# A two-layer attention and expert kernel: the split of the row maxima moves from VectorE to GpSimd, and product slices change places

## What is computed

```python
x = x + layernorm(attn(layernorm(x)))      # 16 heads of 16, causal, window of 250 keys
x = x + layernorm(ffn(layernorm(x)))
# ffn(src): second attention (16 heads, no mask, k and v by way of 64 columns)
#   x  = rmsnorm(src + attention @ Wo) * norm1_w
#   shared = swiglu(x @ W_shared_in) @ W_shared_out
#   w  = weights of the two best of 4 experts in the chosen group of 2
#   h  = swiglu(x @ W1_shared);  routed = sum_e (h @ W2_experts[e]) * w[:, e]
#   out = rmsnorm(x + shared + routed) * norm2_w
```

## Time and profile before

| | us |
|---|---|
| runs of the kernel before | 1979.39, 1984.70, 1986.41 |
| median | 1984.70 |
| the profiled execution's own time | 1978.52 |
| its span | 1976.8 |

### The profile page before, as it was taken

The page is one execution under the profiler, slowest core; times in us unless marked ns, Lnnn a source line. Parts: engine busy times, 40 slices in busy tenths (PEclk is TensorE's granted clock), DMA queues, the critical chain, the costliest instruction groups (busy, mean ns, idle before and its releaser), DMA issues.

```text
span 1976.8 us, 27875 instructions
## 1 busy us (share of the span) xinstructions
PE 1833.7 (93%) x9216; PEld 1022.6 (52%) x9216; DVE 1345.6 (68%) x4116; ACT 807.6 (41%) x1730; POOL 382.1 (19%) x671
## 2 busy tenths in 40 slices
PE   7968899989999999999999999998999999999988
PEld 4343464636555364644637355463645537364466
DVE  6457474775768668685876857677586856868466
ACT  3433535245343634335353353425534363443510
POOL 2336024101231013200251011410123101320010
PEclk8585999999999999999999999899999999999999
DMA  3026002201031100401022010220103110040240
GB/s 110 2 84 236 23 22 87 86 2 54 23 139 44 44 22 13 163 20 48 29 97 87 2 54 23 97 85 2 54 23 139 44 44 23 26 157 1 97 170 11
DMA packets 31295, 123.04 MB, mean 62 GB/s; under 512 B 5424, under 2 KB 18352, under 8 KB 26544
## 3 DMA queue, kind: packets, MB, share of 16 engines
q1 hardware_dynamic: 28624, 105.54, 14.9%
q0 software_dynamic: 2528, 15.73, 2.1%
HBM read 101.33 MB, written 18.87 MB: 61 GB/s over the span
## 4 chain that ended last, share of the span: by engine, by line
PE 74%; DVE 17%; issue 5%; ACT 3%; DMA 1%; POOL 0%; SPq 0%; DVEq 0%; ACTq 0%; POOLq 0%
PE fb L852 12%; PE ot L791 10%; PE sm L750 8%; PE fb L830 6%; DVE negmax L1232 6%; PE st L777 5%; PE fb L826 4%; PE st L718 3%; PE dn L718 3%; PE fb L848 3%; PE st L734 3%; DVE sm L1229 2%; DVE acc L1430 2%; PE sm L777 2%; PE ot L718 2%
## 5 line engine op out<-in xcount | busy, mean ns | idle before, releaser
L630 ACT ACTIVATE probs<-st 128x512 f32<-128x512 f32 (+3 forms) x832 | 395.4, 507 | 388.1 <-PE st L777 384.4
L852 PE MATMUL fb<-w_r,h_r 128*128 128x512 f32 x1344 | 391.5, 418 | 0.0
L750 PE MATMUL sm<-k_t,q_t 48*128 48x512 f32 (+3 forms) x864 | 313.8, 447 | 63.8 <-DVE negmax L1229 31.1
L1232 DVE TENSOR_REDUCE negmax<-sm 128x1 f32<-128x512 f32 x416 | 268.8, 685 | 83.5 <-PE sm L750 83.4
L777 PE MATMUL st<-q_t,k_t 64*128 64x512 f32 (+3 forms) x832 | 298.7, 453 | 22.3 <-ACT probs L630 19.9
L750 PEld LDWEIGHTS sm<-k_t,q_t 48*128 48x128 f32 x864 | 144.5, 195 | 315.3 <-DVE negmax L1229 136.5
L852 PEld LDWEIGHTS fb<-w_r,h_r 128*128 128x128 f32 x1344 | 231.0, 189 | 92.3 <-issue 56.3
L1229 DVE CUSTOM_DVE_ANT_0 sm<-sm,mask_qk 128x384 f32<-128x384 f32 (+1 forms) x448 | 202.1, 469 | 94.6 <-PE sm L750 91.5
L791 PE MATMUL ot<-probs,v_s 128*32 128x512 f32 (+3 forms) x2048 | 252.7, 536 | 2.9 <-POOL probs L505 2.9
L464 POOL TENSOR_TENSOR stack<-rot,stack 128x256 fp32r<-128x256 f32 x64 | 50.0, 782 | 980.7 <-ACT stack L566 980.7
L777 PEld LDWEIGHTS st<-q_t,k_t 64*128 64x128 f32 x832 | 133.6, 193 | 122.4 <-ACT probs L630 88.0
(11 more groups left out here) (214 smaller groups left out, 2589.9 us busy)
## 6 DMA issues: line engine op xcount, KB each, us to landing
w_r<-w_parts SPq DMA_DIRECT2D x30, 2048.0 KB, 8.0
wup_r<-wup_parts SPq DMA_DIRECT2D x32, 512.0 KB, 4.0
w_parts<-w_r POOLq DMA_DIRECT2D x4, 2048.0 KB, 9.4
x_s<-in_L_attn_query SPq DMA_DIRECT2D x8, 512.0 KB, 4.7
q_t<-rot_b SPq DMA_DIRECT2D x256, 4.0 KB
x_kept<-o_s SPq DMA_DIRECT2D x8, 512.0 KB, 3.0
h_s<-in_L_ffn_W_experts POOLq DMA_DIRECT2D x8, 512.0 KB, 5.3
xa<-x_kept SPq DMA_DIRECT2D x8, 512.0 KB, 3.3
```

Source lines behind the costliest of these rows:

```text
L630: nc.scalar.activation(probs[:, n % PSLOTS, 0:hi - lo], score_bank(m)[:, 0:hi - lo], ACT.Exp, scale=float(D) ** -0.5).then_inc(s_ex, 1)
L750: mm(max_bank(w, a)[:, 0:hi - lo], q_t[r:r + MROW, b, t * P:(t + 1) * P], k_t[r:r + MROW, b, lo:hi], start=True, stop=True).then_inc(s_sm, 1)
L852: last = mm(fb[q % 2][:, :], h_r[:, h, m, rows], w2_r[:, k % 2, w, m, :], start=(m == 0 and n == 0), stop=(m == NH - 1 and n == 2))
L1232: return v.tensor_reduce(negmax[:, g % 2, n // GH, c:c + 1], max_bank(g * UNITS + n, a)[:, 0:hi - lo], AX.X, ALU.max, negate=True).then_in ...
```

## The change

Four edits are made together. The bodies of `max_unit`, `score_unit` and the others stay as they are.

1. From batch 1 on, GpSimd splits the maxima. In the first attention it does group 0 ahead of its masks and groups 1 to 3 behind the mask of units 16g + 2 and 16g + 3; in the second attention it does all four in a row, behind its last low parts. DVE keeps the split in batch 0 only. DVE now waits, ahead of the first unit of groups 2 and 3, for the split two groups back.
2. QUIET_OUT: in groups 1 to 3 of the second attention a slice stands behind step 3 and no longer behind step 2; the reading of the block that ends there moves by one step too.
3. The evenly spread slices end at step 0 and no longer at step 1, and the first slice of block 7 takes the place of the two unread products ahead of the second projections; so 9 and no longer 12 products stand behind the second projection.
4. STEPS_AT_LAST is 9, 9, 4, 4, 4, 4 for the six hidden blocks of the drain that have steps behind them (9 each before). Behind the shared blocks it stays 9.

```diff
-QUIET_OUT = [g * UNITS + n for g in range(NGR) for n in ((2, 8, 12) if g else (3, 8, 12))]
+QUIET_OUT = [g * UNITS + n for g in range(NGR) for n in (3, 8, 12)]
...
-OUT_HEADS = {0: ((), (), slices(18, 0, 2), slices(18, 2, 3), slices(18, 3)), 1: ((), slices(7), (), slices(8, 0, 2), slices(8, 2))}
-OUT_AT = [-LEAD] + spread(len(OUT_BESIDE) * NH - len(QUIET_OUT) - 1, 1 - LEAD, 1) + QUIET_OUT
+OUT_HEADS = {0: ((), (), slices(18, 0, 2), slices(18, 2, 3), slices(18, 3)), 1: ((), slices(7, 1), (), slices(8, 0, 2), slices(8, 2))}
+OUT_AT = [-LEAD] + spread(len(OUT_BESIDE) * NH - len(QUIET_OUT) - 1, 1 - LEAD, 0) + QUIET_OUT
...
-STEPS_AT_LAST, STEPS_BESIDE_LAST = 9, 9
+STEPS_AT_LAST, STEPS_BESIDE_LAST = (9, 9, 4, 4, 4, 4), 9
...
+            def split_max(i, a, gr):
+
+                count = (i - 1) * N_MS + a * NGR + gr + 1
+                pool.wait_ge(s_mx, i * N_MX + (a * NGR + gr + 1) * UNITS)
+                if gr >= 2:
+                    pool.wait_ge(s_mp, i * N_MP + a * NGR + gr - 1)
+                m = negmax[:, gr % 2].rearrange("p t (b h) -> p h b t", b=2)
+                hi = m_split[:, gr % 2, :, 0]
+                lo = m_split[:, gr % 2, :, 1]
+                g.tensor_copy(hi, m).then_inc(s_mh, 1)
+                pool.wait_ge(s_mh, count)
+                g.tensor_tensor(lo, m, hi.bitcast(F32), ALU.subtract).then_inc(s_ms, 1)
...
                     last.then_inc(s_mk, 1)
+                    if f is not None and m % UNITS == 2 and m // UNITS + 1 < NGR:
+                        split_max(i, 0, m // UNITS + 1)
...
                 rows_low(i - 1, i * N_SP + 16)
+                split_max(i, 0, 0)
                 mask_probs(i, i - 1)
                 low_parts(i, 1)
+                for gr in range(NGR):
+                    split_max(i, 1, gr)
...
                 if f is not None:
-                    unread(st[1], 2)
+                    expert_out(f, 7, 0)
...
-                        take_max(i, a, *divmod(m + LEAD, UNITS))
+                        gr, n = divmod(m + LEAD, UNITS)
+                        if f is not None and gr >= 2 and n == 0:
+
+                            dve.wait_ge(s_ms, i * N_MS + a * NGR + gr - 1)
+                        take_max(i, a, gr, n)
...
-                    if (m + LEAD) % UNITS == UNITS - 1 and m + LEAD < ALL:
+                    if f is None and (m + LEAD) % UNITS == UNITS - 1 and m + LEAD < ALL:
                         split_max(i, a, (m + LEAD) // UNITS)
...
                 if n < 2 * NH - 2:
-                    for _ in range(STEPS_AT_LAST):
+                    for _ in range(STEPS_AT_LAST[n]):
                         next(others, None)
...
-                for _ in range(STEPS_AT_LAST):
+                for _ in range(STEPS_AT_LAST[0]):
                     next(others, None)
```

More of the change, by code:

```diff
@@ L227, in build @@
         s_ms, N_MS = sem("max_split"), 2 * NGR
+        s_mh = sem("max_high_made_by_pool")
         s_mp, N_MP = sem("max_transposed"), 2 * NGR
```

## The result

| | before | changed |
|---|---|---|
| median of the runs, us | 1984.7 | 1975.7 |
| lowest to highest, 9 runs each | 1973.40 to 1990.02 | 1968.65 to 1976.45 |
| ratio, 95% interval | | 0.9948 (0.9930 to 0.9967) |
| the profiled execution's own time | 1978.52 | 1976.10 |
| its span | 1976.8 | 1974.2 |

A forecast was written before the change was run, and what follows sets the result against it. PE was taken as the bound, delayed by DVE at places, in all by 56 us of 1976.8. Seven blocks gave -1.0 us and the drain -2.6, so -3.6 from the median of 1984.7: 1981.1 us, range 1967 to 1991.

The forecast's parts named there:

- Split: Moving the split of the maxima from DVE to GpSimd: -0.64 us a block, range -0.8 to +0.2.
- The 0.34 us twice: Second attention, groups 0 and 1: each split on DVE delays PE by 0.34 us, 0.68 a block.
- The Trainium skill's rule: GpSimd and VectorE share an SBUF read port, so moving the split might bring nothing; the prediction did not follow it.
- Slice for the unread products: Ahead of the second projections a slice fills the hole, leaving 9 products behind: -0.67 us a block, range -0.7 to -0.3.
- Quiet steps: Second attention, slices moved behind steps 19, 35 and 51 no longer cover waits: +0.38, +0.42 and +0.36 us a block.
- Block: Sum of the split, the slice for the unread products and the three moved slices: -0.15 us, -1.0 over seven blocks.
- Drain: Fewer steps behind hidden blocks, so the shared blocks and then the routed products start earlier: -2.6 us, range -4.6 to 0.
- far value: Drain, DVE's centring step behind the shared blocks: up to 0.67 us each; the near value chosen was 0.43.
- The clock: Rival: the granted clock falls behind new gaps in the second attention, in three blocks at step 51; 2001.5 us, chance 0.10.
- I add the difference to the median: Last step of the sum: the profiled execution, 6.2 us under the median, is forecast at 1974.9, so the median at 1981.1.
- DVE counts for more: Rival: half of the 29 us of DVE's splits comes back as well, giving 1966.6 us; chance 0.22.
- GpSimd late in all groups: Rival: GpSimd's split delays the transposes, the split term becomes +0.2 and the first attention loses 0.2 to 0.4; 1989.5 us, chance 0.10.

The follow-up runs named there:

- a1: The changed kernel with the split of all maxima back on DVE; median 1984.9 us, ratio 0.9996 to the kernel before.
- b2: The kernel before with the split of the maxima on GpSimd and nothing else changed; median 1983.1 us, ratio 0.9988 to the kernel before.
- c3: The kernel before with only the change's drain steps (9, 9, 4, 4, 4, 4); median 1980.1 us, ratio 0.9987 to the kernel before.
- b4: The changed kernel with GpSimd splitting in the second attention only, DVE in the first; median 1976.6 us, ratio 0.9952 to the kernel before.

## Why the prediction was right, and where it was not

- **Split, -0.64 a block: -0.66**, measured twice (a1 against changed, b2 against before). The 0.34 us twice, and no gain in the first attention, hold. GpSimd's two instructions take 0.20 and 0.22 us beside DVE's maxima, and two of these take 1.28 us beside them as without. The Trainium skill's rule that spoke against it (Perfetto Trace Analysis, section Optimizing Scalar/DVE Operations) does not decide here, by these rows.
- **Slice for the unread products, -0.67: -0.34.** The term that was mis-sized. The hole and the 9 products are as worked out, but "what follows is PE's chain and then the rotation on DVE, which waited for PE" took the rotation at its old length. Moved 0.7 us forward it runs beside GpSimd and takes 1.00 instead of 0.69 us. The weak end of the range (-0.3) is what came.
- **Quiet steps, +0.38, +0.42, +0.36: +0.33, +0.35, +0.12.** The first two hold. The third was mis-sized: "ACT, which was behind, absorbs half" was too little, it absorbed most.
- **Block**: -0.66 - 0.34 + 0.80 is -0.20, and the periods of before and after differ by 0.33; the 0.13 between may be the last spread slice, which had no kernel of its own. Seven blocks are -2.3 us by the steady period and some -1.9 added up, not -1.0. That the total came so near is in part luck: the unread slice brought 0.33 us a block less than forecast, the third quiet step cost 0.24 less, and the spread slice had been given nothing of its own.
- **Drain, -2.6: -2.7**, with its parts: 0.85 us of idle time for 0.9, 1921.26 for 1921.3, 0.42 for a centring step, a clock of 1.00. c3 shows it alone. The prediction's far value for such a step, 2.69 / 4 = 0.67, was a mean of unlike ones. In the trace of before three take 0.41 us, and one, beside a subtraction of GpSimd, 1.34:

```profile
1909.12 1.27 POOL L493 TENSOR_TENSOR h_r<-sg,h_r 128x512 fp32r<-128x512 f32 x1 [2.68 <-ACT h_r L566]
1909.19 1.34 DVE L1190 TENSOR_SCALAR acc<-acc,mv,rstd 128x256 f32<-128x256 f32 x1
```

GpSimd's last subtraction of the changed drain is over at 1914.66, before the steps at 1917.93, so the near value that was chosen holds.

- **The clock.** It stood in the prediction only as a rival in which it falls. The step that failed is the last of the sum, "I add the difference to the median": it took for granted that runs of the changed kernel would lose as much to falls of the clock as runs of before, which puts 6.2 us between the profiled execution and the median. The changed kernel's nine runs lie from 1968.65 to 1976.45, with the profiled one at 1976.1. So of the 9 us some 4 to 5 are order and the rest clock. For the profiled execution 1974.9 was forecast and 1976.1 came, which is luck: the first batch was 9.1 us longer than before's, and before's two falls, some 7 us, were missing. The rival had the clock as a cause of its own, with the wrong sign: of the three places that it feared (gaps at steps 19, 35 and 51) none shows a fall in the changed kernel, though the gaps are there.
- **"DVE counts for more"** (1966.6) fell: the split gives 4.6 us and no more, the first attention nothing. **GpSimd late in all groups** fell, but its sign shows in part: before the transposes of the first attention's last group and the second's first PE's weight loads sit idle for 0.39 to 0.40 us until GpSimd is done, 13 times in the program, 5.1 us in all. In the first attention that group's transpose comes 0.2 us later than before (41.52 against 41.32), and b4, which has DVE there, is only 0.04 us a block shorter; so almost all of it is hidden.

## What to carry to other kernels

Work out an edit at the instruction that is late, block by block, and then check it with a ruler: the start of one rare instruction in every block shows 0.1 us where run times scatter by 10. A slice that stands in a wait for another engine was free here, and one step later it cost 0.12 to 0.35 us, least where ACT caught up most; an instruction that is moved forward gets new neighbours, so look at what runs on the other engines where it lands. Where the granted clock falls now and then, compare its mean over many runs of each kernel beside the time, and don't explain the difference of two medians by the order of instructions alone.

## What the runs showed of the hardware

- DVE's addition of 128 x 512 with two inputs takes 0.69 us alone and 1.00 to 1.18 beside a GpSimd subtraction. A centring step of 128 x 256 takes 0.41 us alone and 1.34 when it starts 0.07 us behind a GpSimd subtraction of 1.27. DVE's maxima of 128 x 512 (one input) are as long beside GpSimd's small split as without it (two in 1.28 us).
- GpSimd's copy and subtraction of 128 x 16 take 0.20 and 0.22 us; on DVE they take 0.18 each.
- The granted clock falls in steady work of a program whose order is fixed, at one place of the block above all, in some blocks and some runs only. A long fall, with two stretches of 10 us at 0.68 and 0.63, costs 4.5 to 4.9 us. At that place it was seen in 7 of 42 blocks of six kernels, and in none of 56 blocks of eight kernels whose PE stopped less there.
- In the drain the granted clock was 0.79 over the 8 us behind stops of PE of 1.83, 1.96, 3.29, 3.45 and 3.55 us, and 1.00 behind stops of 1.37 to 1.70.
- Within each kernel, 0.001 of mean granted clock went with 1.36 us of a span of some 1975.
